# Grouped attention in a two-layer decoder: query/key weights rotated by TensorE, the mask applied as a factor, softmax sums taken by products with ones, X loaded ahead of the tables

## The reference, cut to what matters

```python
q = (x @ wq.T + bq) ; k = (x @ wk.T + bk) ; v = (x @ wv.T + bv)   # 512, 128 and 128 wide
q, k = rope(q), rope(k)          # cos*t + sin*rotate_half(t), angle taken by head number
s = q @ k.T / sqrt(32) + tril    # tril is 1 where key <= query, else 0: added, not -inf
p = softmax(s)
x = layernorm(x + (p @ v) @ wo.T + bo)
```

## Time and profile before

| | |
|---|---|
| time, median of 3 runs | 2207.17 us (2204.45 to 2207.64) |
| the profiled execution's own time | 2212.43 us |
| its span, first to last instruction | 2210.6 us |
| mean granted TensorE clock | 0.953 |
| PE busy in the span | 1988.7 us, 90% |
| DVE, ACT, POOL busy | 1074.2, 708.0, 344.3 us |
| the grouped phase | first DMA at 5.3 us, the next phase's first DMA at 303.0 us |

### The profile page before, as it was taken

The page is one execution under the profiler, slowest core; times in us unless marked ns, Lnnn a source line. Parts: engine busy times, 40 slices in busy tenths (PEclk is TensorE's granted clock), DMA queues, the critical chain, the costliest instruction groups (busy, mean ns, idle before and its releaser), DMA issues. The chain is left out here.

```text
span 2210.6 us, 32808 instructions
## 1 busy us (share of the span) xinstructions
PE 1988.7 (90%) x12204; PEld 1617.5 (73%) x12204; DVE 1074.2 (49%) x1892; ACT 708.0 (32%) x2271; POOL 344.3 (16%) x308
## 2 busy tenths in 40 slices
PE   5999968999999988999889997999978999899991
PEld 4777646778888866777668876677766777799990
DVE  5566734345545446433454446577765232222226
ACT  1555622334333432211131111344541121233332
POOL 1111100000000008200020000000002300544415
PEclk9899968999999999999989999999988999999996
DMA  5011133000000004000084001000013300444236
GB/s 187 11 30 40 40 143 113 33 1 1 1 1 1 1 5 153 1 0 0 0 304 154 1 1 48 20 1 1 1 43 119 115 1 0 178 163 158 77 110 200
DMA packets 61437, 135.90 MB, mean 61 GB/s; under 512 B 6256, under 2 KB 24048, under 8 KB 59376
## 3 DMA queue, kind: packets, MB, share of 16 engines
q1 hardware_dynamic: 36240, 94.14, 12.1%
q0 software_dynamic: 5840, 27.92, 3.6%
q10 hardware_dynamic: 19216, 11.89, 1.9%
HBM read 90.68 MB, written 43.25 MB: 61 GB/s over the span
## 5 line engine op out<-in xcount | busy, mean ns | idle before, releaser
L1245 PE MATMUL banks<-ternary_xth,ternary_wq 128*128 (+1 forms) x352 | 139.8, 397 | 6.1 <-DVE ternary_wq L1175 4.8
L1245 PE MATMUL banks<-ternary_xtl,ternary_wq 128*128 (+1 forms) x352 | 138.3, 393 | 0.0
L97 PE MATMUL banks<-latent_vh,latent_cth 128*128 128x512 f32 x256 | 104.8, 409 | 3.5 <-DVE latent_ctl L951 3.5
L97 PE MATMUL banks<-weights,expert_xgh 128*128 x312 | 104.7, 336 | 2.4 <-DVE expert_xgl L1797 2.4
L433 ACT ACTIVATE gqa_pr<-banks,gqa_nb 128x128 f32<-128x128 f32 x256 | 89.9, 379 | 51.6 <-DVE gqa_nb L569 51.6
L433 ACT ACTIVATE causal_pr<-banks,causal_nb 128x128 f32<-128x128 f32 x256 | 89.9, 380 | 50.8 <-DVE causal_nb L569 50.8
L98 PE MATMUL banks<-weights,expert_xgh 128*128 x312 | 101.3, 325 | 0.0
L99 PE MATMUL banks<-weights,expert_xgl 128*128 x312 | 101.3, 325 | 0.0
L98 PE MATMUL banks<-latent_vl,latent_cth 128*128 128x512 f32 x256 | 100.4, 392 | 0.0
L99 PE MATMUL banks<-latent_vh,latent_ctl 128*128 128x512 f32 x256 | 100.1, 391 | 0.0
L1204 DVE TENSOR_TENSOR ternary_hf<-ternary_sg,banks 128x512 f32<-128x512 f32 x44 | 30.2, 687 | 133.7 <-issue 80.1
(11 more groups left out here) (427 smaller groups left out, 5562.2 us busy)
## 6 DMA issues: line engine op xcount, KB each, us to landing
x_slots<-decay_zeros SPq DMA_DIRECT2D x39, 256.0 KB, 3.0
y_slots<-decay_zeros SPq DMA_DIRECT2D x39, 256.0 KB, 3.3
expert_xin<-x_slots SPq DMA_DIRECT2D x39, 256.0 KB, 3.3
y_slots<-expert_ys SPq DMA_DIRECT2D x39, 256.0 KB, 2.1
weights_raw<-in_expert_experts SPq DMA_DIRECT2D x4, 2176.0 KB, 8.8
gqa_tw<-in_ternary_w ACTq DMA_DIRECT2D x4, 2112.0 KB, 10.8
ternary_raw<-in_ternary_w SPq DMA_DIRECT2D x11, 768.0 KB, 4.2
expert_raw<-in_expert_experts POOLq DMA_DIRECT2D x3, 2176.0 KB, 9.8
```

Of the source, the lines that this page charges most:

```text
L97: pe.matmul(out, wh, xh, start=first, stop=False, **kw)
L1245: a = pe.matmul(dst[:, :], wq[:, j, m, c * P:(c + 1) * P], x[:, c, toks], start=c == 0 and n == 0, stop=c == C - 1 and n == 1)
```

## The change

1. X of the first group (four DMAs) and the query weights (four) are issued by SP in the first block; the six tables move to ACT's queue, which waits for them there.
2. The query and key weights come in untransposed. PE multiplies them by small rotation matrices (`turn_q`, 128x640): 16 products of 128x128 into banks 0 to 3 and 4 into bank 4. That transposes and rotates at once. ACT and DVE split straight from the banks. `rotate` is gone, and so is the 128x1280 table.
3. The mask is not added any more. DVE multiplies the transposed exponentials by `factor` (e where the key is at or before the query, else 1) while it takes them from the bank.
4. The sums come from four products of a 128x32 tile of ones with P^T, a new banked entry "sum", after which DVE takes the reciprocal of 128x512 from the bank. ACT's running sums, the small reciprocal, POOL's spreading, PE's transposes of it and ACT's copy are gone from this phase.
5. POOL's code for the first bias additions is rewritten. The v and o weights are loaded as soon as the weights are turned. DVE's `split_q` waits for the small loads behind the splits, in all three attention phases.

```diff
-                        plan += [("T", b - 1, 1), ("rec", b - 1, 0)]
+                        plan.append(("T", b - 1, 1))
+                        if kind == "causal":
+                            plan.append(("rec", b - 1, 0))
...
                     if h == 1 and 1 <= b <= B:
+                        if kind == "gqa":
+                            plan.append(("sum", b - 1, 0))
                         plan.append(("pv", b - 1, 0))
...
+            def bias_row(b, h):
+                pool.wait_ge(pp_full, place[("x", b, h)] + 1)
+                row = S.X[:, GT * b + h, :]
+                pool.tensor_tensor(out=row, in0=row, in1=bor[:, :], op=ALU.add).then_inc(x_biased, 1)
+
+            for k, (what, b, h) in enumerate(plan):
+                if bias and (what, b, h) == ("S", 0, 0):
+                    for _, g, i in [e for e in plan[:k] if e[0] == "x"]:
+                        bias_row(g, i)
...
+                for c in range(C):
+                    dve.wait_ge(wq_hi, c + 1)
+                    if kind == "gqa":
+                        whole = S.bank[c]
+                    else:
+                        dve.wait_ge(wq_in[c], 16)
+                        whole = ws[0][:, c * DM:(c + 1) * DM]
+                    dve.tensor_tensor(wql[:, c, :], whole, f32(wqh[:, c, :]), ALU.subtract).then_inc(wq_lo, 1)
                 if n_loads:
                     dve.wait_ge(const_in, 16 * n_loads)
...
+                    if kind == "gqa":
+                        each = factor[:, :].unsqueeze(1).broadcast_to((P, 8, P))
+                        dve.tensor_tensor(pt[:, b % 2, 8 * h:8 * h + 8, :], unit_banks(2), each, ALU.mult).then_inc(pt_done, 1)
...
+                elif what == "sum":
+                    dve.reciprocal(rts[:, :], bank).then_inc(free_d, 1)
...
+            def turn_weights():
+                pe.wait_ge(turn_in, 16)
+                for c in range(C):
+                    for j in range(C):
+                        if c == 0:
+                            pe.wait_ge(wq_in[j], 16)
+                        m = pe.matmul(S.bank[c][:, j * P:(j + 1) * P], ws[0][:, j * DM + c * P:j * DM + (c + 1) * P],
+                                      turn_q[:, j, :], start=True, stop=True)
+                    m.then_inc(ws_turned, 1)
...
-                        for x in range(2):
-                            pe.matmul(S.bank[2 * h + x], identr[:, :], maskr[:, :].unsqueeze(1).broadcast_to((P, 4, P)),
-                                      start=True, stop=False)
...
+                elif what == "sum":
+                    pe.wait_ge(pt_done, 2 * b + 2)
+                    for r in range(4):
+                        m = pe.matmul(bank[D * r:D * r + D, :], S.ones_f[:, 0:D], pt[:, b % 2, 4 * r:4 * r + 4, :],
+                                      start=True, stop=True)
```

More of the change, by code:

```diff
@@ L280, in attention_phase @@
                 j -= 1
-        banked = [e for e in plan if e[0] in ("x", "c", "q", "k", "v", "rt", "pv", "out")]
+        banked = [e for e in plan if e[0] in ("x", "c", "q", "k", "v", "rt", "sum", "pv", "out")]
         place = {e: k for k, e in enumerate(banked)}
@@ L304, in tokens @@
             return slice((b % GT) * P, (b % GT + 1) * P)
-        n_loads = 3 * bias + 3 * (kind == "gqa") + (kind == "decay")
+        n_loads = 3 * bias + 2 * (kind == "gqa") + (kind == "decay")
         blocks = ExitStack()
@@ L344, in _ @@
                 pool.wait_ge(const_in, 16 * n_loads)
[L345 to L349, removed]
+            def bias_row(b, h):
[6 more added lines that the diff above has]
+                        bias_row(g, i)
+                if what == "x" and bias and k > plan.index(("S", 0, 0)):
+                    bias_row(b, h)
                 elif what == "rec":
@@ L600, in _ @@
         def _(pe):
+            def turn_weights():
[7 more added lines that the diff above has]
+                    m.then_inc(ws_turned, 1)
+                pe.wait_ge(ws_in[1], 16)
+                for c in range(C):
+                    m = pe.matmul(S.bank[4][:, c * P:(c + 1) * P], ws[1][:, c * P:(c + 1) * P], turn_q[:, C, :],
+                                  start=True, stop=True)
+                m.then_inc(ws_turned, 1)
             for e in plan:
@@ L621, in _ @@
                 elif what in "qk":
+                    if kind == "gqa" and (what, b, h) == ("q", 0, 0):
+                        turn_weights()
                     if h == 0:
@@ L640, in _ @@
                 elif what == "S":
-                    if u == 0 and soft:
+                    if u == 0 and kind == "causal":
                         pe.wait_ge(const_hi, 2)
@@ L1946, in build @@
         loaded, S.ones_set = ctx.enter_context(nc.semaphore("tables_in")), ctx.enter_context(nc.semaphore("ones_set"))
+        S.x0_in = [ctx.enter_context(nc.semaphore(f"x0_in{i}")) for i in range(GT)]
+        S.wq_in = [ctx.enter_context(nc.semaphore(f"wq_in{c}")) for c in range(C)]
+        first = ctx.enter_context(ExitStack())
+        S.ws = first.enter_context(nc.sbuf_tensor("first_ws", [P, 2, C * DM], F32))
         tables = [(S.ident, a[""]["ident"]), (S.tril, a[""]["tril"]), (S.upper, a[""]["upper"]), (S.causal, a[""]["causal"]), (S.dist, a[""]["dist"]), (S.iota, a[""]["iota"])]
@@ L1950, in _ @@
             def _(sp):
+                for i in range(GT):
+                    sp.dma_start(S.X[:, i, :], S.x_dram[:, i, :]).then_inc(S.x0_in[i], 16)
+                for c in range(C):
+                    sp.dma_start(S.ws[:, 0, c * DM:(c + 1) * DM], a["attn0"]["q"][:, c, :]).then_inc(S.wq_in[c], 16)
+            @block.scalar
+            def _(act):
                 for dst, src in tables:
-                    sp.dma_start(dst[:, :], src).then_inc(loaded, 16)
-                sp.wait_ge(loaded, 16 * len(tables))
+                    act.dma_start(dst[:, :], src).then_inc(loaded, 16)
+                act.wait_ge(loaded, 16 * len(tables))
             @block.vector
@@ L1962, in build @@
             attention_phase(nc, S, "gqa", a["attn0"])
+            first.close()
         if phases >= 2:
```

120 lines of the change are left out of this document (59 added, 61 removed).

## The result

| | before | changed |
|---|---|---|
| time, median | 2207.4 us (2204.45 to 2207.64) | 2236.42 us (2233.77 to 2238.4), 4 runs |
| ratio, 95% interval | | 1.013 (1.0112 to 1.0148) |
| span of the profiled execution | 2210.6 us | 2235.3 us |
| mean granted TensorE clock | 0.953 | 0.945 |

The change is slower by 1.3%, 29 us; the two profiled executions differ by 24.7 us. The forecast was 2224 us with its own range 2212 to 2240. I read the same views again.

What follows compares the result with a forecast made beforehand. PE's own queue bounds the kernel, DVE's chain the last four blocks. Start -12, decay -3, blocks +24 and clock +7 sum to +16: 2224 us as the median, own range 2212 to 2240, overall range 2202 to 2242.

Steps and rivals of the forecast that it cites:

- The reciprocal: DVE's 128x512 reciprocal in each grouped block takes 3.3 us, by the slope of 8- and 16-element rows.
- rival 3: Grouped blocks: reciprocal takes eight steps per element, 4.4 us, 1.1 us more per block, +17, 2241 us; chance 0.09.
- Rivals 1: Grouped blocks: reciprocal streams at 0.68 us, no PE wait, no clock loss, 2184 us; chance 0.15.
- Rival 2: No change: blocks lose 24 but clock stays up, starts bring 15 and 5; 2211 us or less; chance 0.10.
- The P^T multiplication: DVE's multiplication of P^T by the factor in grouped blocks costs what the copy did, 1.22 us.
- The wait and PE's gain: Per grouped block PE waits 1.55 us for the reciprocal and saves 0.65 us of work: +0.9 us.
- The clock: Falls to half clock at about five waits, around X tiles and in the last blocks: +7 us, bounds 0 and 14.
- The blocks: Grouped phase's periods, last two outputs and -1 before the first output: +24 us together, without clock loss.
- The X tiles: Two grouped periods with X tiles, which DVE reaches 3.3 us later: +2.3 us each, +4.6.
- The last periods: Three periods of the last grouped blocks, where DVE's chain is the path: +2.5 us each, +7.5.
- The start: Kernel start: first projection at 21 us, keys at 32 instead of 43.67; -12 us, bounds -8 and -15.
- The decay phase: Decay phase: query splits on DVE come ahead of the slopes' wait, PE starts earlier; -3 us, bounds 0 and -5.

Runs made afterwards that it cites:

- experiment 5: New blocks of the change (factor multiplication, ones-products, wide reciprocal) with start, loads and decay phase of the kernel before: 2249.4 us, 1.0174 of the kernel before.
- experiments 1: Changed kernel with DVE copying the sums out of their bank instead of taking their reciprocal: 2182.74 us, 0.9884 of the kernel before.
- 8: Changed kernel with the reciprocal moved from DVE to ScalarE as exp(-ln), ones-products ahead of the second half's scores: 2186.21 us, 0.9898 of the kernel before.
- 2: Changed kernel plus six useless mask products on PE ahead of the first scores of each block from the second on: 2225.52 us, 1.0088 of the kernel before.
- experiment 10: Changed kernel with ScalarE copying the sums' bank to SBUF, DVE's reciprocal reading that copy at its same place: 2244.8 us, 1.0165 of the kernel before.
- experiment 4: Changed kernel's start, loads and waits with the blocks of the kernel before (additive mask, running sums, spreading): 2190.37 us, 0.9929 of the kernel before.
- 9 on it: Kernel of experiment 4 with the identity loaded first, other loads behind, ScalarE's table load early: 2187.52 us, 0.9913 of the kernel before.
- 9 on 8: Kernel with exp(-ln) on ScalarE, plus identity loaded first, other loads behind, ScalarE's table load early: 2173.99 us, 0.9854 of the kernel before.
- experiment 7: Changed kernel with early sums copied by ScalarE and raised to -1 by GpSimd instead of DVE's reciprocal: 3453.42 us, 1.563 of the kernel before.

## Why the prediction was right, and where its terms were off

- **The reciprocal.** Forecast 3.3 us, measured 3.348. The slope of the two narrow forms held: (3348 - 243) / 496 = 6.26 ns per element. With rival 3's eight steps it would have been 4.4 us. Rivals 1 and 3 fell here. Rival 2 needed a clock that stays up, and it fell in nearly every block.
- **The P^T multiplication** like the copy: 1.22 forecast, 1.221 measured.
- **The wait and PE's gain.** Forecast 1.55 and -0.65 us, +0.9 a block; 1.64 measured, and +0.98 (16.15 against 15.17 at the same place) in the blocks of experiment 5 whose clock stayed up. The mechanism is shown by experiments 1 and 8, and its part in the clock by 2; experiment 10 corrects its wording: the time in DVE's row, and only in small part the bank.
- **The clock** is the term that was mis-sized. I placed the 1.64-us waits between one idle time that brought a fall and one that did not, and counted about five falls at the X tiles and late blocks, +7 of 0 to 14. In the changed kernel nearly every block had one: 51 us more at half clock between the first and last output add. The fall in experiment 5's second block lasted 3.4 us and cost 1.57; at that price the 51 us come to 24, an estimate, and far above the 14 that I had as the bound. The blocks were forecast at +25 and the clock at +7; they measured +44 together, which leaves about 20 for the blocks. The X tiles are where these were too high: +1.8 each with all it holds, where I had +2.3 without a fall. The last periods were +4.0 to +4.9, which is my +2.5 and a fall, or a little more.
- **The start** was too hopeful in its reason. Tables that share the engines were put at 1 or 2 us; the phase began at 10.10 us, and X's first split was at 13.8, not 10. Turning took 7.4 us for all 40 records (6.7 for the query weights), forecast 7. So the first projection came at 25.18, forecast 21; the query products then took the 11 us forecast, and the keys began at 36.18, forecast 32. By the keys the start had won 7.5 us, outside its bounds of 8 to 15. The first output came 10.8 us sooner, forecast 13 (12 for the start, 1 for the blocks): the other 3.3 us came between keys and first output, where only 1 was counted, and brought the term back inside its bounds by luck. In that stretch the kernels with 10.2 us at half clock (experiment 4, and 9 on it) won 3.4 us, and those with 3.4 us at half clock (experiment 5, and 9 on 8) won 8.4 and 8.9.
- **The decay phase:** -3 forecast, -2.9 measured, and 262.6 us without the edit.
- **Not in the forecast:** latent became 5.3 us shorter. In the thirteen traces its length goes with its time at half clock: 517.7 to 518.7 us with 31 to 41 us of it in nine, 521.9 with 50.9, 522.4 with 54.8, 523.69 with 52.7, 525.25 with 57.6. What sets that time stays open.
- **The sum.** -10.8 + 44.1 - 0.3 - 5.3 - 0.8 - 2.9 + 0.7 = +24.7, forecast +16. The clock was some 17 us too low and the blocks some 5 too high, 12 together; the start gave 2 less than forecast, and 5 of latent that I had not counted made up for part of it. Between the medians the change is +29 and not +24.7, as the profiled execution of before stood above its median. 2224 was 12 us low, and 2236 lies in the range of 2212 to 2240: the mechanism was right, but that its largest miss stayed inside is in part luck.

## What to carry to other kernels

Before an operation moves to a wide form on an engine with free time, work out its time from the slope between two widths of that same operation, and look at what stands behind it in that engine's row: 3.35 us of DVE, with a third of its time free, cost 54 us in sixteen blocks against a copy of 0.68 us. A wait that opens in every block of a kernel bound by TensorE was priced twice here, once for itself and once for the clock, so ask where useful or even useless work can stand in it. Freeing the buffer moved the wait to the next one here; taking the operation to an engine that idled there removed it.

## What the runs showed of the hardware

- A float32 reciprocal on DVE costs 6.26 ns per element of a row (3348 ns for 512, 243 for 16), from PSUM or SBUF alike (3352 ns from SBUF).
- GpSimd's power costs 160 ns per element (81.9 us for 128x512), 64 times a 128x512 add (1.27 us; the expectation of experiment 7 has 1.24).
- The same wait of 1.64 us left the clock at 1.00 in one block and halved it in another with the same instructions, for 1.57 us.
- Useless products in the idle time made a kernel 11 us faster by the medians (9 by the ratios).
- Ln and Exp in turn on ScalarE took two table loads of 1.28 us a block. The Trainium skill (ScalarE: Activation LUTs, "Table sets: the hidden batching unit") has a set with both functions and counts one load for ln and then exp; the two loads a block in this trace show that it was not used. Between the end of the Ln and the start of the Exp lay 1.31 us.
- A 4-KB load issued behind five tables and beside 2 MB on another queue landed after 6.6 us; behind the same tables and ahead of the 2 MB, after 2.0.
